# A scan kernel's last batch: three of VectorE's products by C's row given to GpSimd, and the gathers dealt anew

## What is computed

```python
dA = jnp.exp(jnp.einsum('bti,is->btis', delta, A))            # 256 channels i, 16 states s
dBu = jnp.einsum('bti,bts->btis', delta * u, B_ssm)
def step(h, inp):
    dA_t, dBu_t, C_t = inp
    h = dA_t * h + dBu_t
    y_t = jnp.einsum('bis,bs->bi', h, C_t)
    return (h, y_t)
...
y = (ys.transpose(1, 0, 2) + u * D_param) * silu(z)
return y @ out_proj_w.T + residual
```

## Time and profile before

| what | us |
|---|---|
| median of 3 runs | 619.3 |
| lowest and highest | 616.77, 620.64 |
| the profiled execution | 621.67 |
| its span, first to last instruction | 619.8 |
| batch 7's first scan begins, in the span | 553.94 |
| its last product ends | 613.67 |

### The profile page before, as it was taken

The page is one execution under the profiler, slowest core; times in us unless marked ns, Lnnn a source line. Parts: engine busy times, 40 slices in busy tenths (PEclk is TensorE's granted clock), DMA queues, the critical chain, the costliest instruction groups (busy, mean ns, idle before and its releaser), DMA issues.

```text
span 619.8 us, 11393 instructions
## 1 busy us (share of the span) xinstructions
PE 544.9 (88%) x3554; PEld 426.3 (69%) x3554; DVE 590.9 (95%) x852; ACT 455.4 (73%) x916; POOL 497.6 (80%) x395
## 2 busy tenths in 40 slices
PE   4989878888989999899989899899999797778887
PEld 2377767646788777787778778877777465657564
DVE  6989969998999999999999999999999998999997
ACT  1798787138876798677986798867986579969881
POOL 5697059448999799997999979998898976885684
PEclk9979878987999999999999999999999999988999
DMA  7430209824777888778869788688994345432364
GB/s 201 143 118 1 72 2 201 284 76 155 226 243 266 265 307 270 259 243 279 287 229 320 241 286 273 229 272 287 285 285 169 149 155 210 143 99 83 97 137 91
DMA packets 60893, 122.99 MB, mean 198 GB/s; under 512 B 8218, under 2 KB 41378, under 8 KB 53794
## 3 DMA queue, kind: packets, MB, share of 16 engines
q1 hardware_dynamic: 53826, 112.42, 54.1%
q0 software_dynamic: 6288, 9.52, 7.1%
q10 hardware_dynamic: 720, 0.33, 0.2%
HBM read 112.77 MB, written 9.47 MB: 197 GB/s over the span
## 4 chain that ended last, share of the span: by engine, by line
PE 41%; DVE 18%; ACT 17%; issue 14%; POOL 8%; DMA 2%; DVEq 0%; ACTq 0%; POOLq 0%
PE bank L1421 7%; PE bank L1572 7%; DVE bank L1134 6%; PE bank L1455 5%; DVE h_sb L1151 5%; PE bank L1586 5%; POOL dbu L920 4%; PE bank L1580 4%; ACT dbu L531 3%; ACT da L503 3%; ACT bank L515 2%; PE bank L1478 2%; PE bank L1384 2%; PE bank L1470 1%; POOL xs L908 1%
## 5 line engine op out<-in xcount | busy, mean ns | idle before, releaser
L920 POOL TENSOR_TENSOR dbu<-du,xn_all 128x1024 f32<-128x1024 f32 x86 | 203.8, 2370 | 32.6 <-DVE bank L1134 32.0
L1134 DVE TENSOR_TENSOR_SCAN bank<-bank,dbu 128x512 f32<-128x512 f32 x170 | 207.3, 1222 | 2.2 <-ACT bank L515 1.7
L1151 DVE TENSOR_TENSOR h_sb<-bank,xh_all 128x512 f32<-128x512 f32 x240 | 159.4, 678 | 1.2
L515 ACT ACTIVATE bank<-delta,a_sb 128x512 f32<-128x512 f32 x170 | 116.6, 688 | 41.4 <-DVE h_sb L1151 39.5
L1421 PE MATMUL bank<-id_sb,h_sb 128*128 128x128 f32 x992 | 135.3, 281 | 12.6 <-DVE h_sb L1151 10.9
L1421 PEld LDWEIGHTS bank<-id_sb,h_sb 128*128 128x128 f32 x992 | 116.0, 146 | 25.0 <-DVE h_sb L1151 17.0
L1134 DVE TENSOR_TENSOR_SCAN bank<-da,bank 128x512 f32<-128x512 f32 x82 | 96.3, 1213 | 10.3 <-PE bank L1384 9.4
L1572 PEld LDWEIGHTS bank<-wd_sb,hid 117*128 117x128 f32 (+1 forms) x432 | 54.7, 190 | 49.4 <-DVE hid L1185 26.0
L1572 PE MATMUL bank<-wd_sb,hid 117*128 117x128 f32 (+1 forms) x432 | 64.1, 284 | 18.6 <-ACT xT L692 18.5
L908 POOL DMA_INDIRECT xs<-xn_rows,src x72 | 70.0, 973 | 12.4 <-issue 9.1
L531 ACT ACTIVATE dbu<-du_t,bc_sb 128x256 f32<-128x256 f32 x164 | 69.5, 496 | 11.1 <-PE bank L1384 8.1
(11 more groups left out here) (197 smaller groups left out, 898.3 us busy)
## 6 DMA issues: line engine op xcount, KB each, us to landing
xh_all<-b_rows SPq DMA_DIRECT2D x30, 1024.0 KB
xn_all<-b_rows SPq DMA_DIRECT2D x25, 1024.0 KB
wgu_sb<-in_w_gu SPq DMA_DIRECT2D x72, 352.0 KB
wd_sb<-in_w_dn SPq DMA_DIRECT2D x72, 192.0 KB
y_slots<-ys SPq DMA_DIRECT2D x72, 64.0 KB
xn_rows<-xn_all SPq DMA_DIRECT2D x2, 1040.0 KB, 10.4
out<-x_sb SPq DMA_DIRECT2D x7, 256.0 KB
x_sb<-in_x SPq DMA_DIRECT2D x2, 640.0 KB, 6.0
```

The source lines that it names most:

```text
L515: nc.scalar.activation(bank_of(b, m)[:, :], delta[b % 2][:, hf, :], ACT.Exp, scale=a_sb[:, hf, k:k + 1]).then_inc(s["da_rdy"], 1)
L920: nc.gpsimd.tensor_tensor(dbu[k % 2][:, :, :], du[b % 2][:, :, :], b_ring[c % 2][:, k % CH, :].unsqueeze(1).to_broadcast([P, NH, T]), ALU. ...
L1134: nc.vector.tensor_tensor_scan(at, da_of(n)[:, hf, :] if n in IN_SBUF else at, inp, 0.0, ALU.mult, ALU.add).then_inc(s["h_rdy"], 1)
L1151: nc.vector.tensor_tensor(h_sb[k % 2][:, hf, :], bank_of(b, 2 * k + hf)[:, :], row, ALU.mult).then_inc(s["p_rdy"], 1)
```

## The change

In states 1, 3 and 5 of batch 7 VectorE's two products are left out. The scans of these states write a spare buffer in SBUF (`sp_d`, `sp_y`, `sp_d`) instead of their bank. GpSimd multiplies both halves at once by C's row into `h_sb[1]` (`row_product`, a 128x1024 product that waits for both scans and for the sum of the state two before) and raises a semaphore of its own, `pp_rdy`. PE sums these states later in its step, behind the turn for the next state and the step's other work, and waits for `pp_rdy`. Whoever counted `p_rdy` now counts VectorE's products alone, or both semaphores, and whoever waited for a bank whose state is one of the three waits for its scan. The table deals GpSimd's gathers of batch 7 anew: the 16 of the first kind in steps 0 to 7, the 16 of the second in steps 8 to 13.

```diff
+        MULTIPLIED = [7 * S + k for k in (1, 3, 5)]
+        KEPT = (sp_d, sp_y)
+        def kept(n):
+            return KEPT[MULTIPLIED.index(n) % len(KEPT)]
+        def by_pool(m):
+            return sum(2 * n < m for n in MULTIPLIED)
+        def by_vector(m):
+            return m - sum(min(max(m - 2 * n, 0), 2) for n in MULTIPLIED)
+        def multiplied(eng, m):
+            wait(eng, "p_rdy", by_vector(m))
+            wait(eng, "pp_rdy", by_pool(m))
+        def bank_read(eng, m):
+            if (m - 1) // 2 in MULTIPLIED:
+                wait(eng, "h_rdy", m)
+            else:
+                wait(eng, "p_rdy", by_vector(m))
...
-                7: [2, 2, 3, 2, 2, 3, 2, 2, 3, 2, 3, 2, 2, 2, 0, 0]}
+                7: [2, 1, 3, 1, 3, 1, 3, 2, 3, 3, 3, 3, 2, 2, 0, 0]}
...
+            def row_product(n):
+                b, k = n // S, n % S
+                c = k // CH
+                row = c_ring[c % 2][:, k % CH, :]
...
+                wait(pool, "acc_mm", 2 * (n - 1))
+                pool.wait_ge(s["h_rdy"], 2 * n + 2)
+                nc.gpsimd.tensor_tensor(h_sb[k % 2][:, :, :], kept(n)[:, :, :], row.unsqueeze(1).to_broadcast([P, NH, T]),
+                                        ALU.mult).then_inc(s["pp_rdy"], 1)
...
             def gathers(b, k):
                 for i, ((b0, c), t) in enumerate(ADD_AT[b * S + k]):
-                    if i == 0:
+                    if i == 0 or S * b + k in MULTIPLIED:
                         pool.wait_ge(s["h_rdy"], 2 * (S * b + k) + 1)
                     else:
-                        pool.wait_ge(s["p_rdy"], 2 * (S * b + k) + i)
+                        pool.wait_ge(s["p_rdy"], by_vector(2 * (S * b + k) + i))
...
+                    if b * S + k in MULTIPLIED:
+                        row_product(b * S + k)
                     if b >= 5:
                         gathers(b, k)
...
-                nc.vector.tensor_tensor_scan(at, da_of(n)[:, hf, :] if n in IN_SBUF else at, inp, 0.0,
+                out_at = at
+                if n in MULTIPLIED:
+                    out_at = kept(n)[:, hf, :]
+                    if hf == 0:
+                        kept_free(n)
+                nc.vector.tensor_tensor_scan(out_at, da_of(n)[:, hf, :] if n in IN_SBUF else at, inp, 0.0,
                                              ALU.mult, ALU.add).then_inc(s["h_rdy"], 1)
...
             def product(b, k, hf):
+                if b * S + k in MULTIPLIED:
+                    return
...
-                wait(pe, "p_rdy", 2 * (n + 1))
+                if n in MULTIPLIED:
+                    wait(pe, "pp_rdy", by_pool(2 * n + 2))
+                else:
+                    wait(pe, "p_rdy", by_vector(2 * (n + 1)))
...
-                if k > 0:
+                if k > 0 and g - 1 not in MULTIPLIED:
                     accumulate(g - 1)
...
                 if b == NB - 1 and k in (13, 14):
                     last_parts(k - 13)
+                if k > 0 and g - 1 in MULTIPLIED:
+                    accumulate(g - 1)
```

More of the change, by code:

```diff
@@ L198, in build @@
                    exp_rt x_pad acc_w g_mm u_mm bct_rdy dbu_p row_mm dbu_0 b_st b_in0 b_in1 c_in0 c_in1
[L199 removed]
+                   br_mm dbu_rdy da_rdy h_rdy p_rdy pp_rdy acc_mm y_out dd_rdy xc_mm x_th x_half u_rdy v_mm
                    v_out bc_mm bc_rdy z_mm z_rdy z_one o_ev sp_exp sp_ln sp_rem sp_w sp_sum z_th delta_rdy du_rdy
@@ L352, in out_rows_in @@
             def out_rows_in(b, c):
-                wait(sp, "p_rdy", 2 * S * b + 2 * CH * (c - 1) if b else 0)
+                if b:
+                    multiplied(sp, 2 * S * b + 2 * CH * (c - 1))
                 spread_rows(c_ring[c % 2], b * 2 * S + S + c * CH, CH).then_inc(s[f"c_in{c % 2}"], 16)
@@ L445, in softplus @@
             if b == 1:
-                eng.wait_ge(s["p_rdy"], 8)
+                multiplied(eng, 8)
             for hf in halves:
@@ L509, in decay_bank @@
                 m = 2 * k + hf
-                wait(act, "p_rdy", freed(b, m))
+                bank_read(act, freed(b, m))
                 if b == 6 and m == 2:
@@ L724, in half_tanh @@
                 if c == 2:
-                    act.wait_ge(s["p_rdy"], 16)
+                    multiplied(act, 16)
                 at = u_sb[c % 3][:, hf, :]
@@ L922, in scaled @@
                                         ALU.mult).then_inc(s["dbu_p"], 1)
+            def row_product(n):
+                b, k = n // S, n % S
+                c = k // CH
+                row = c_ring[c % 2][:, k % CH, :]
+                if b == 0 and c < 2:
+                    pool.wait_ge(s[f"c_own{k // 2}"], 16)
+                    row = own[k // 2][:, k % 2, :]
+                else:
+                    pool.wait_ge(s[f"c_in{c % 2}"], 16 * ((b - 1) * 2 + c // 2 + 2) if b else 16)
+                wait(pool, "acc_mm", 2 * (n - 1))
+                pool.wait_ge(s["h_rdy"], 2 * n + 2)
+                nc.gpsimd.tensor_tensor(h_sb[k % 2][:, :, :], kept(n)[:, :, :], row.unsqueeze(1).to_broadcast([P, NH, T]),
+                                        ALU.mult).then_inc(s["pp_rdy"], 1)
             def step(b, k):
@@ L1114, in _, with kept_free @@
             rows_normed(TT, XH_HEAD)
+            def kept_free(n):
+                wait(dve, "pp_rdy", MULTIPLIED.index(n) - len(KEPT) + 1)
+                dve.wait_ge(s["delta_rdy"], 2 * NB)
             def scan(b, k, hf):
@@ L1132, in scan @@
                 elif b == NB - 1 and k == 1:
-                    wait(dve, "p_rdy", 2 * S * b + 1)
-                nc.vector.tensor_tensor_scan(at, da_of(n)[:, hf, :] if n in IN_SBUF else at, inp, 0.0,
+                    wait(dve, "p_rdy", by_vector(2 * S * b + 1))
+                out_at = at
[4 more added lines that the diff above has]
+                nc.vector.tensor_tensor_scan(out_at, da_of(n)[:, hf, :] if n in IN_SBUF else at, inp, 0.0,
                                              ALU.mult, ALU.add).then_inc(s["h_rdy"], 1)
@@ L1139, in product @@
                 c = k // CH
+                if b * S + k in MULTIPLIED:
+                    return
                 if b == 0 and c < 2:
-                    if k % 2 == 0 and hf == 0:
+                    if hf == 0:
                         dve.wait_ge(s[f"c_own{k // 2}"], 16)
@@ L1144, in product @@
                 else:
-                    if k % CH == 0 and hf == 0:
+                    if hf == 0 and (k % CH == 0 or b * S + k - 1 in MULTIPLIED):
                         dve.wait_ge(s[f"c_in{c % 2}"], 16 * ((b - 1) * 2 + c // 2 + 2) if b else 16)
@@ L1380, in dbu_turn @@
                 for hf in halves:
-                    wait(pe, "p_rdy", freed(b, 2 * k + hf))
+                    bank_read(pe, freed(b, 2 * k + hf))
                     at = bank_of(b, 2 * k + hf)
@@ L1396, in input_turn @@
                     pe.wait_ge(s["o_rdy"], b - 1)
-                    wait(pe, "p_rdy", 2 * b * S - 2)
+                    bank_read(pe, 2 * b * S - 2)
                 for i in range(2):
@@ L1410, in accumulate @@
                     for hf in range(NH):
-                        wait(pe, "p_rdy", 2 * n + hf + 1)
+                        wait(pe, "p_rdy", by_vector(2 * n + hf + 1))
                         MM(YB[hf][:, :], id_sb[:, :], h_sb[k % 2][:, hf, :], start=False, stop=(k == S - 1),
@@ L1562, in slots_turn @@
                 if j == 0:
-                    pe.wait_ge(s["p_rdy"], 2 * S - 2)
+                    bank_read(pe, 2 * S - 2)
                 nc.tensor.transpose(XD[:, 0:P], xs[j % NXS][:, 0:H], id_sb[:, :]).then_inc(s["xt_mm"], 1)
```

1 line of the change is left out of this document (removed).

## The result

The changed kernel takes 621.15 us, the median of 20 runs (618.5 to 623.9), against 618.46 us for 20 runs of the kernel before on the same chip (616.51 to 620.64). The ratio is 1.0042, with a 95% interval of 1.0027 to 1.0057: slower by 2.6 us (1.7 to 3.5), where +0.9 was forecast. Its profiled execution took 623.02 us with a span of 621.2, against 621.67 and 619.8.

The account below looks back on a forecast made before the run. VectorE's chain ended last, with GpSimd's gather queue almost as late. Gathers 3.3 us later against 2.55 room put the last outputs 0.8 later, plus 0.1 collision: 619.3 + 0.9 = 620.2 us, range 616.8 to 622.6.

Parts of the forecast that it names:

- GpSimd's queue sets it, +0.4 to +1.8 with 0.60: Likeliest case: at the kernel's end, GpSimd's late gathers delay the outputs, +0.4 to +1.8 us; chance 0.60.
- GpSimd's new work: Batch 7, GpSimd: three added products, each 2.37 + 0.16 us, 2.25 net, 6.75 together; last gather ends 3.3 us later.
- the walk's 0.95: Timeline of GpSimd's queue in batch 7: the gather behind state 1's product and scan takes 0.95 us, no longer 1.59.
- State 1, gain 0: Batch 7, state 1: dropping VectorE's products gains 0, since state 2's scans need PE's turns, which come no earlier.
- States 3 and 5, gains 0.4 and 1.0: Batch 7, VectorE: dropped products gain 0.4 us in state 3 and 1.0 in state 5; chain ends about 1.4 earlier.
- Scans into SBUF as long as into PSUM: States 1, 3 and 5: scans writing SBUF take 1.12 us as into PSUM, bounds 0.1 less or more each.
- PE hidden by 0.8 to 1.7 us: States 1, 3 and 5: GpSimd's products finish before PE's later sums need them, with 0.8 to 1.7 us of cover.
- The last outputs 0.8 later: SP at the end: batch 4's output 3.3 us later against 2.55 room, so the last two outputs go 0.8 later.
- The room is 3.00 us less one issue on SP: 2.55 us: SP's queue: batch 4's output could slip 2.55 us (617.13 - 614.13, less 0.45) before delaying the last two outputs.
- VectorE's chain didn't set the end: Concerns the rival that VectorE's chain still sets the end: gain of 0.5 to 3.6 us, -1.4 by the walk; chance 0.17.
- Nothing moves: Rival at the kernel's end: room and delay cancel within half a microsecond, time stays 619.3 us; chance 0.13.
- PE waits for GpSimd's products: Rival in batch 7: late GpSimd products hold PE's sums, turns and next scans, giving 621.5 to 622.5 us; chance 0.10.

Follow-up runs that it names:

- e7_before_gathers_into_batch6: The kernel before with six of batch 7's gathers dealt into batch 6, without the products on GpSimd; ratio to the kernel before 1.0032.
- e12_before_four_gathers: The kernel before with four of batch 7's gathers dealt into batch 6, the deal alone; ratio to the kernel before 1.0088.
- the freed pair: The changed kernel and the kernel before, each with six of batch 7's gathers dealt into batch 6; ratios to the kernel before 1.0012 and 1.0032.
- the control: The kernel before, unchanged, timed as the experiments were; ratio 0.9988, from 0.9966 to 1.0011.
- e13_last_four_gathers_left_out: The changed kernel without its last four gathers; no ratio given, drain ended at 62.85 us, VectorE's last adding 4.5 us later than in the changed kernel.
- e8: The changed kernel with six gathers dealt into batch 6, and states 3, 5, 7 and 9 moved instead of 1, 3 and 5; ratio 1.0061.
- e3: The changed kernel with SP sending batch 7's two last outputs ahead of batch 4's; ratio to the kernel before 1.0029 [1.0007, 1.0051].
- e10: The kernel before with one unused 128x1024 product on GpSimd behind its last gather; ratio to the kernel before 1.0034.
- e5: The changed kernel with six of batch 7's gathers dealt into batch 6; ratio to the kernel before 1.0012 [0.9988, 1.0037].
- e11: The changed kernel with states 3 and 5 alone on GpSimd and four gathers dealt into batch 6; ratio to the kernel before 1.0052.

## Why the prediction was right on the side and short on the size

**What sets the end: right engine, wrong instruction of it.** GpSimd's queue sets it, +0.4 to +1.8 with 0.60; measured +2.6 (1.7 to 3.5), more than this case allowed for. Of the forecast's steps one failed, the last. The median came closer (620.2 forecast, 621.15 measured) than the change did, by luck: the 619.3 that the forecast was counted from, a median of 3 runs, lies 0.8 above that of 20, 618.46.

**GpSimd's new work: right.** Three products of 2.36 to 2.38 us and 0.16 behind each, with 2.37 taken. From batch 7's first scan, the first gather into `x_sb` is 3.50 us later than before, the last one's end too, with 3.3 forecast at an unchanged pitch. The gather behind state 1's product took 0.98, the walk's 0.95. The prediction left two reasons for the long gather of before, the scan beside it, whose two inputs are both in SBUF, and the pause ahead of it. The profiles settle that. In `e7_before_gathers_into_batch6` a gather beside that scan takes 1.77 us though only 0.30 us idle stand before it (556.84); in `e12_before_four_gathers` one behind a pause of 2.84 us, beside a scan that reads a bank, takes 0.94 (573.59). So it is the scan. This agrees with the rule of the Trainium skill's page SBUF — State Buffer (Who interferes with whom) that the prediction cites.

**State 1, gain 0: right, at the lower clock.** State 3 starts 12.76 us after the batch's first scan in both kernels; in the freed pair it is 11.79 in both. In these four profiles the granted clock of the stretch of 5 us looked at in the last section is 0.68 to 0.74. At 1.00 it isn't so: state 3 starts at 12.19 in the control and at 11.71 in `e13_last_four_gathers_left_out`, which has the product of state 1 moved, and the step of state 1 takes 3.43 and 2.98. There the product gives some 0.45 us. VectorE's rows in the changed kernel, which answer to the earlier trace rows:

```profile
558.17 2.33 DVE L1189 TENSOR_TENSOR_SCAN sp_d<-da,dbu 128x512 f32<-128x512 f32 x2
562.01 1.23 DVE L1189 TENSOR_TENSOR_SCAN bank<-da,bank 128x512 f32<-128x512 f32 x1 [1.51 <-ACT da L531]
563.72 1.23 DVE L1189 TENSOR_TENSOR_SCAN bank<-da,bank 128x512 f32<-128x512 f32 x1 [0.48 <-PE bank L1441]
564.86 1.27 DVE L1208 TENSOR_TENSOR h_sb<-bank,xh_all 128x512 f32<-128x512 f32 x2
566.04 2.32 DVE L1189 TENSOR_TENSOR_SCAN sp_y<-da,bank 128x512 f32<-128x512 f32 x2
568.31 1.23 DVE L1189 TENSOR_TENSOR_SCAN bank<-da,bank 128x512 f32<-128x512 f32 x1
570.04 1.23 DVE L1189 TENSOR_TENSOR_SCAN bank<-da,bank 128x512 f32<-128x512 f32 x1 [0.50 <-PE bank L1441]
```

The 1.18 us of the two products became idle time in front of state 2's scans: 1.51 + 0.48 against 0.25 before. The rest of that, some 0.6, is there because state 1 itself began 0.64 earlier behind the batch's first scan (4.89 against 5.53). The first of the two waits is put down to ACT's exp(delta A), which ended at 561.97, only 0.07 behind PE's turn (561.90); the prediction had named the turn alone.

**States 3 and 5, gains 0.4 and 1.0: right in sum.** Two steps took 7.44 us before. Now states 3 and 4 take 6.92 (gain 0.52), 5 and 6 6.73 (0.71). Together VectorE's chain gains 1.23 with 1.4 forecast; its last adding is at 61.51 instead of 62.74 (62.17 in the control), and PE's second turn is where it waits, 0.50 in the last row above. The 0.4 for state 3 has a slip in it: by its own walk PE is 0.2 late (568.2 for 568.01), so the turn ends at 570.6 and not at 570.75, and the gain is 0.5.

**Scans into SBUF as long as into PSUM: right.** 2.32 or 2.33 for two in the rows above, the same as for two into a bank.

**PE hidden by 0.8 to 1.7 us: right.** No sum waits for GpSimd: the three products end 2.4, 1.25 and 0.8 us before PE begins the sum of their state. In e8, where the cover is gone, one does, and it costs 4.59.

**The last outputs 0.8 later: right.** 617.45 from the batch's first scan is 64.17, against 63.19 before: +0.98. The output of batch 4 was the last thing ahead of them. From there on 0.28 more are lost (SP is done 1.26 later, not 0.98), where the forecast had +0.1 for a collision on the DMA engines; no run shows whether it is that.

**"The room is 3.00 us less one issue on SP: 2.55 us": here it failed.** This term measures from the last gather to the last outputs. There is a second way from the last gather to the end, which doesn't pass SP: GpSimd's drain. Before, it ended at 618.14 in a span of 619.8, so the room to the end was 1.66 us; the forecast's 2.55 to the last outputs, and what follows these until the end, lay on the other way. With the term in the right size the same sum reads: last gather 615.80, drain 5.65 behind it, 0.2 to the end, 621.65; against 619.8 that is +1.9, and 619.3 + 1.9 = 621.2 us. Measured: 621.15, which fits so closely by luck, since 619.3 is 0.8 too high. Counted from the batch's first scan the end moved +2.06 against the profile of before and +2.53 against the control's. Of the 2.06, 1.26 come by the way through SP that the forecast counted (66.92 against 65.66); the drain, which it left out, adds 0.8.

The row was there to be read. The chain of waits ends at VectorE's last adding and at SP's outputs, and the prediction went on from it by the two queues' timelines, in which the drain isn't a row. It shows in the view of L56. Two runs hold this against the forecast's version: with the outputs sent ahead of batch 4's (e3) the end doesn't move, and with one instruction more behind the last gather (e10) the drain ends as much later.

**The rivals.** VectorE's chain didn't set the end; freed of GpSimd it would have given 1.1 us (e5 against e7), not the full 3.54. "Nothing moves" was refuted by the interval. PE waits for GpSimd's products at no place of this change.

## What to carry to other kernels

Before work is moved onto an engine that isn't on the chain of waits, read when each engine is done with its drain, and take the room from that, since the engine's last instruction isn't its end. Count a dealt queue by what each piece has to wait for: work in its idle time is nearly free, as state 1's product was, and the same work a few steps on costs most of its length (with states 3 and 5 alone the last gather ends 3.75 us later, for two products of 2.25 net). And what is moved to an earlier stage stands in front of something there; look first for the piece of that queue which another engine waits for.

## What the runs showed of the hardware that was not expected

GpSimd's drain ends 5.6 to 5.7 us behind its last instruction's row in eleven of the fourteen profiles (6.0 in e11, 5.3 in e13, 8.00 behind the gather and 5.6 behind the product in e10), though the last gather's data is there 1.7 us behind its row: batch 4's output follows at 617.03 in after, and the row ended at 615.32. The Trainium skill's Perfetto Trace Analysis page (DMA Instruction, SWDGE), by which such a row ends when the last descriptor is written, covers the 1.7 us and not the rest. The row of SP's drain is 7 ns long, that of VectorE's 464 ns, that of GpSimd's 11,840 ns in before: 6.2 us of it pass while GpSimd's gathers are still at work, 5.65 us behind the last of them.

The kernel before, run twice, shows two ways through states 0 to 2 of batch 7. The stretch of 5 us that begins 8.1 us behind the batch's first scan, in the profile of the kernel before and then in that of the control (columns: stretch, its length, busy time of PE, PEld, VectorE, ACT and GpSimd, granted clock, DMA share, GB/s):

```profile
562.00:567.00 5.00, 5.00 (x34) 4.71 (x33) 4.75 (x7) 4.24 (x10) 2.99 (x4) 0.74 0.15 43
```

```profile
559.10:564.10 5.00, 4.67 (x38) 3.92 (x37) 5.00 (x7) 4.75 (x11) 3.15 (x4) 1.00 0.17 43
```

At a mean granted clock of 0.74, partly the lower of the two levels (1.2 GHz), PE is busy all the time and VectorE waits for it 0.25 us; at 1.00 VectorE waits for nothing. State 2 takes 3.79 us at 0.74 and 3.42 at 1.00; in `e7_before_gathers_into_batch6`, with 0.73 in the same stretch, it takes 3.72. So 0.3 to 0.4 us of this stretch go with the clock. Another 0.2 are lost in state 0, ahead of it (5.53 against 5.34), and state 3 starts 12.76 instead of 12.19 us after the first scan. In the changed kernel the clock is 0.68 there; with the same products moved and 1.00 (e13) state 3 starts at 11.71. One profile against one other can't be read more finely than these 0.6 us.

The same stream of instructions lost 3.1 us in steps 7 to 11 of batch 6 in e12 and not in e7, and 2.4 us in e11 and not in e5, though the kernels of each pair differ only behind that place. In e13 VectorE stood 3.08 us for a releaser without a name, and GpSimd and PE stood behind it, waiting for its product. Both were seen; neither was explained.
